# Stage two of an adapter feed-forward kernel: another order on VectorE and ScalarE, and residual rows loaded two chunks later

## The reference

```python
# x (8, 256, 1024); ids (8,), each 3 to 7; weight (8, 1024, 1024)
x1 = einsum('bsi,boi->bso', x, weight[ids])                 # stage one
base_out = einsum('btd,od->bto', x1, base_W) + base_b
logits = einsum('btd,nd->btn', x1, router_W) + router_b     # 15 logits
probs = softmax(logits)
topk_p, topk_i = top_k(probs, 8)
w = topk_p summed by expert_map[topk_i]                     # 8 experts
h = einsum('btd,erd->bter', x1, A)                          # 8 experts x rank 16
lora = einsum('bter,eor->bto', h * w[..., None], Bm) * 2.0
out = x + base_out + lora
```

## Time and profile before

| | us |
|---|---|
| median of 3 runs | 430.16 (429.05 to 432.26) |
| the profiled execution, its own time | 432.55 |
| its span | 430.7 |
| TensorE busy | 404.3 |
| VectorE busy | 295.6 |
| ScalarE busy | 154.9 |

### The profile page before, as it was taken

One profiled execution on the slowest core, in us unless ns is written; L12 is line 12 of the kernel. 1 busy time (PEld: TensorE's weight loads), 2 busy tenths in 40 slices (PEclk: granted clock), 3 DMA queues, 4 the chain that ended last, 5 costly groups with the idle time before them and its releaser, 6 DMA issues.

```text
span 430.7 us, 6373 instructions
## 1 busy us (share of the span) xinstructions
PE 404.3 (94%) x2272; PEld 373.5 (87%) x2272; DVE 295.6 (69%) x577; ACT 154.9 (36%) x238; POOL 0.8 (0%) x8
## 2 busy tenths in 40 slices
PE   6989969998599998999999999999999999999997
PEld 5869869877598898989899898988989898988996
DVE  2586996788736886389844998369863898449643
ACT  3466325571104631166202642056401652035200
POOL 0000000000000000000000000000000000000000
PEclk9999999999599999999999999999999999999999
DMA  6999403771015740276204760157402762055002
GB/s 200 384 299 390 151 1 148 266 226 45 0 50 202 284 147 0 97 278 219 88 0 174 282 226 0 49 218 269 146 0 110 289 211 72 0 195 195 2 2 97
DMA packets 25598, 64.73 MB, mean 150 GB/s; under 512 B 2546, under 2 KB 11634, under 8 KB 25586
## 3 DMA queue, kind: packets, MB, share of 16 engines
q1 hardware_dynamic: 25586, 64.57, 42.4%
HBM read 56.18 MB, written 8.39 MB: 150 GB/s over the span
## 4 chain that ended last, share of the span: by engine, by line
PE 61%; DVE 21%; ACT 6%; issue 6%; DMA 5%; SPq 1%; DVEq 0%; ACTq 0%
PE y_ps L726 22%; PE y_ps L728 11%; DMA w_raw<-in_wT 5%; PE x_ps L761 4%; PE x_ps L763 4%; PE x_ps L762 4%; DVE w_lo L458 3%; ACT w_hi L357 3%; DVE res L555 3%; DVE x_split L464 3%; ACT x_split L367 1%; PE y_ps L738 1%; PE z_ps L762 1%; PE z_ps L761 1%; PE z_ps L763 1%
## 5 line engine op out<-in xcount | busy, mean ns | idle before, releaser
L726 PE MATMUL y_ps<-x_split,w_hi 128*128 128x512 f32 x496 | 173.1, 395 | 3.1 <-DVE y_sum L470 2.9
L728 PE MATMUL y_ps<-x_split,w_lo 128*128 128x256 f32 x496 | 137.6, 277 | 0.0
L726 PEld LDWEIGHTS y_ps<-x_split,w_hi 128*128 128x128 f32 x496 | 93.0, 188 | 25.6 <-issue 3.1
L728 PEld LDWEIGHTS y_ps<-x_split,w_lo 128*128 128x128 f32 x496 | 93.2, 188 | 0.0
L458 DVE TENSOR_TENSOR w_lo<-w_raw,w_hi 128x1024 fp32r<-128x1024 f32 x62 | 75.7, 1224 | 16.5 <-ACT w_hi L357 14.4
L357 ACT CAST w_hi<-w_raw 128x1024 fp32r<-128x1024 f32 x62 | 64.8, 1049 | 14.4 <-DMA w_raw<-in_wT 14.3
L349 ACT COPY y_sum<-y_ps 128x256 f32<-128x256 f32 x62 | 23.1, 372 | 115.7 <-PE y_ps L728 115.7
L470 DVE TENSOR_TENSOR y_sum<-y_ps,y_sum 128x256 f32<-128x256 f32 x62 | 26.1, 421 | 30.3 <-ACT y_sum L349 29.7
L749 PE MATMUL pl_ps<-pl_hi,y_hi 128*128 128x432 f32 x128 | 46.0, 359 | 0.0
L750 PE MATMUL pl_ps<-pl_lo,y_hi 128*128 128x432 f32 x128 | 45.8, 358 | 0.0
L751 PE MATMUL pl_ps<-pl_hi,y_lo 128*128 128x432 f32 x128 | 45.8, 358 | 0.0
(11 more groups left out here) (136 smaller groups left out, 608.0 us busy)
## 6 DMA issues: line engine op xcount, KB each, us to landing
w_raw<-in_wT SPq DMA_DIRECT2D x63, 512.0 KB, 3.3
res<-in_x SPq DMA_DIRECT2D x16, 512.0 KB, 4.2
out<-res SPq DMA_DIRECT2D x15, 512.0 KB, 2.6
x_raw<-in_xT SPq DMA_DIRECT2D x14, 512.0 KB, 6.1
hi_raw<-in_base_t SPq DMA_DIRECT2D x4, 368.0 KB, 6.1
st_raw<-in_base_t SPq DMA_DIRECT2D x4, 368.0 KB, 6.8
pl_raw<-in_base_t SPq DMA_DIRECT2D x2, 576.0 KB, 6.4
x_raw<-in_xT SPq DMA_DIRECT2D x4, 256.0 KB, 4.1
```

Of the source, the lines that this page charges most:

```text
L726: nc.tensor.matmul(y_ps[:, c % 2, :], w_hi[:, s, k, :], x_split[:, k, :, :].rearrange("p s t -> p (s t)"), start=(k == 0), stop=False)
L728: mm = nc.tensor.matmul(y_ps[:, c % 2, 0:T], w_lo[:, s, k, :], x_split[:, k, 0, :], start=False, stop=(k == KC - 1))
```

## The change

VectorE, all elements but 0: the low part of next x (`make_x_lo`) moves from before `fourth_lo` to behind `make_hwt_lo`, so `routing_logits` and the first x_ps add come earlier. In element 1, `fourth` and `routing_logits` go ahead of `add_bias`, and `fourth_lo` goes behind `make_hwt_lo`. ScalarE: `exponential` goes ahead of `make_x_hi`. SyncE: the residual rows are loaded with chunks 4 and 5. In element 0 the splits of the A, router and plain columns come two chunks later, the routing comes straight behind the masks, then bias add and block sums 1 and 2, then `make_hwt_lo`, the low part of Bm, block sums 3 and 4, next x, and the next element's weights. TensorE waits for the low parts of T1, T2, T3 one by one instead of for all three ahead of T1's product.

```diff
                         load_w(this if c + W_SLOTS < OC else nxt, (c + W_SLOTS) % OC)
-                    if c in (2, 3):
-                        load_res(b, c - 2)
+                    if c in (4, 5):
+                        load_res(b, c - 4)
...
                 fourth_hi(b)
+                exponential(b)
                 if not last:
                     make_x_hi(b + 1)
-                exponential(b)
                 make_hwt_hi(b)
...
-                if c == 2:
+                if c == 4:
                     ar_hi()
-                if c in (3, 4):
-                    plain_hi(c - 3)
+                if c in (5, 6):
+                    plain_hi(c - 5)
             for h in range(2):
                 blocks_hi(h)
+            exponential(0)
             make_x_hi(1)
-            exponential(0)
             act.wait_ge(b_in, 16)
             act.wait_ge(ar_lo_done, 2)
             nc.scalar.copy(b_hi[:, :], b_raw[:, :]).then_inc(b_hi_done, 1)
+            make_hwt_hi(0)
             for c in range(OC, OC + 3):
                 adapter_hi(0, c)
-            make_hwt_hi(0)
...
-            def stage2(b):
-                routing_logits(b)
+            def stage2(b, last):
                 dve.wait_ge(res_biased, 2 * b + 2)
                 dve.wait_ge(x_ps_done, x_adds(b, 1))
                 add(0, N1, x_ps[:, 0:NH]).then_inc(x_added, 1)
...
                 make_hwt_lo(b)
+                if isinstance(b, int) and b == 1:
+                    fourth_lo(b)
+                if not last:
+                    make_x_lo(b + 1)
                 dve.wait_ge(x_ps_done, x_adds(b, 3))
...
                     t2_lo()
                     t34_lo()
-                add_bias(b)
-                fourth(b)
-                if not last:
-                    make_x_lo(b + 1)
-                fourth_lo(b)
-                stage2(b)
+                    fourth(b)
+                    routing_logits(b)
+                    add_bias(b)
+                else:
+                    add_bias(b)
+                    fourth(b)
+                    fourth_lo(b)
+                    routing_logits(b)
+                stage2(b, last)
...
-                if c == 2:
+                if c == 4:
                     ar_lo()
-                if c in (3, 4):
-                    plain_lo(c - 3)
+                if c in (5, 6):
+                    plain_lo(c - 5)
             blocks_lo(0)
             blocks_lo(1)
             masks()
-            block_sums_1_2()
-            add_bias(0)
             routing_logits(0)
             routing_gates(0)
-            make_x_lo(1)
+            add_bias(0)
+            block_sums_1_2()
+            make_hwt_lo(0)
             dve.wait_ge(b_hi_done, 1)
             nc.vector.tensor_tensor(b_lo[:, :], b_raw[:, :], b_hi[:, :], ALU.subtract).then_inc(b_lo_done, 1)
+            block_sums_3_4()
+            make_x_lo(1)
             for c in range(OC, OC + 3):
                 adapter_lo(0, c)
-            make_hwt_lo(0)
-            block_sums_3_4()
...
-                pe.wait_ge(t_lo_done, 3)
+                pe.wait_ge(t_lo_done, 1)
                 pe.wait_ge(s_lo_done, KH * (b - 1) + KH)
                 pe.wait_ge(z_added, z_adds(b, 0))
                 product(z_ps, s_block(S1), T1).then_inc(z_ps_done, 1)
+                pe.wait_ge(t_lo_done, 2)
                 pe.wait_ge(x_added, x_adds(b, 1))
                 product(x_ps, s_block(S2), T2, begins=False).then_inc(x_ps_done, 1)
...
+                pe.wait_ge(t_lo_done, 3)
                 pe.wait_ge(x_added, x_adds(b, 2))
                 product(x_ps, s_block(S3), T3, begins=False).then_inc(x_ps_done, 1)
```

## The result

| | before | after |
|---|---|---|
| median, us | 430.39 (429.05 to 432.26) | 415.64 (414.16 to 417.20) |
| the profiled execution, its own time | 432.55 | 415.91 |
| its span | 430.7 | 414.1 |
| TensorE busy | 404.3 | 403.5 |

The medians are of four runs each (the 430.16 us ahead of the prediction was of three). The ratio is 0.966 with a 95% interval of 0.960 to 0.971: faster by 3.4%, 14.8 us by the medians and 16.6 us by the two profiled executions. The same kernel was run and profiled once more, on another chip: a median of 414.54 us beside 430.57 us, and 413.86 us for its profiled execution. In the code after, the stage-one matmuls are L732 and L734, the plain ones L755 to L757, the block products L767 to L769, `lora_b` L781 to L783; the lines of VectorE and ScalarE keep their numbers up to L564.

What follows compares the result with a forecast made beforehand. TensorE, busy 94% of the span, bounds the kernel: its matmuls plus its holes. Gains of 5.8 + 6.2 + 1.8 + 5.3 = 19.1 us from 430.16 give 411.1 us, range 408.5 to 418.0.

Steps and rivals of the forecast that it cites:

- main case: Whole kernel: all terms as forecast, elements 0 and 1 within their bounds; 409 to 414 us, chance 0.62.
- best bounds: Whole kernel: largest gains allowed, 6.7 us in element 0 and 8.5 us in element 1, giving 408.5 us.
- element 1: Element 1 overall: stalls and slow clock fall from 11.1 to 4.9 us; gain 6.2 us, bounds 1.3 and 8.5.
- element 2: Element 2, before the second x_ps product: the 1.50 us hole goes with 0.26 us restart; gain 1.8 us.
- elements 3 to 6: Before the second x_ps product: the 1.06 us hole goes, 1.32 us in each element; gain 5.3 us.
- Steady elements: Elements 2 to 6: x_ps add at about 212.8, before TensorE wants it; moved make_x_lo hidden behind make_hwt_lo.
- Element 0: Plain products 0.9 us earlier, holes before transposes (1.85) and adapter's second product (3.0) go; 5.8 us, bounds 4.0 and 6.7.
- Element 1, stage one: Stage one of element 1: VectorE about 2 us late; 2.1 us of new holes, bounds 1.2 and 3.0.
- Element 1, S2: Element 1, before the second x_ps product: loss 2.8 us instead of 7.07, bounds 1.4 and 4.0.
- Clock: I take none: Element 1: no slow-clock cost after the change, bounds 0 and 2.78 us; before, 2.78 us.
- Residual loads: SyncE's loads two chunks later: no cost in steady elements; element 1's late chunk 7 weights had cost a 1.0 us hole.
- VectorE becomes the limit between elements 0 and 1: Rival: late stage one 1.2, late weights at plain product 1.2, clock drop 2.8 us; 416.3 us, 414 to 418, chance 0.22.

Runs made afterwards that it cites:

- steady-part kernel: Kernel before with only make_x_lo behind make_hwt_lo and ScalarE's exponential first, in elements 2 to 6; 423.38 us, ratio 0.984.
- two kernels: Kernel after with SyncE's adapter numbers read before waiting for element 0's stores, 412.54 us; that plus element 1's first weight load ahead of the second store, 411.39 us.
- element 0 and residual-load kernels: Kernel before with only element 0's new order, 429.14 us; kernel before with only residual rows loaded with chunks 4 and 5, 432.08 us in one run.

## Why the prediction was right where it was, and where not

The forecast was 411.1 us with a range of 408.5 to 418.0; 415.64 us lies in it. It lies outside the 409 to 414 us of the main case, which had the larger chance, and inside the 414 to 418 us of the second. (The range's lower end has a slip: the best bounds sum to 6.7 + 8.5 + 7.1 = 22.3 us, not 21.6.) The sum was 19.1 us, the two profiles show 16.6. Term by term:

| | predicted, us | measured, us |
|---|---|---|
| element 0 | 5.8 | 68.48 - 63.64 = 4.84 |
| element 1 | 6.2 | 60.00 - 55.27 = 4.73 |
| element 2 | 1.8 | 50.44 - 48.68 = 1.76 |
| elements 3 to 6 | 5.3 | 4 x 1.32 = 5.28 |

The first two terms depend on the execution. The second profile of the unchanged kernel after starts element 1 at 62.14 and element 2 at 116.87, so it has 6.34 and 5.27 us for them, 18.7 us in all. And in the steady-part kernel, whose elements 0 and 1 are those of before, element 0 ends at 71.16 and element 1 takes 57.02 us. By the start of element 2 the kernels with the old elements 0 and 1 agree better (128.2 to 128.5 in four profiles): from 128.48 the two terms together are 9.6 and 11.6 us in the two profiles, forecast 12.0.

- **Steady elements: right.** The step counted what stands between the fourth sum and the add. It had the add at 33.9 us behind the start of stage one (212.8 - 178.92) and it came at 33.8 (201.40 - 167.59). That `make_x_lo` is hidden behind `make_hwt_lo` held as well.
- **Element 0: right in mechanism, 1.0 us too high.** The hole before the transposes and the 2.77 us one are gone; 0.58 us is left before the plain product (1.0 was given back in the sum). Chunk 2 started at 16.41 us, 15.82 before, which is the first DMAs and explains 0.6 us; other executions started element 1 at 62.14 (the same kernel) and 64.00 (with the residual loads put back). Alone, this part gives only 1.7 us by the medians.
- **Element 1, stage one: mis-sized.** The sum had 2.1 us of holes with an upper bound of 3.0; it is 2.91 + 0.26 = 3.2, with clock 4.8 us. "SyncE too sends the second store, and then this element's loads, only after the last add of element 0" named the right queue, but gave the reading of the adapter numbers nothing. Before, it was hidden: the store was issued by 69.6, and the load at 71.7 had in any case to wait for the first chunk, done at 71.4. An earlier TensorE took that cover away. VectorE's lateness was real (first y_sum at 68.67) but was not what ended the hole; it then idled 3.74 us. That shortening SyncE's path shortens the hole, to 1.24 and 0.40 us, is shown by two kernels.
- **Element 1, S2: over-priced.** 2.8 us were taken, 1.48 + 0.26 = 1.7 came. VectorE's chain from the T2 split to the end of the add is as forecast: 107.9 - 97.43 = 10.5 us, measured 105.68 - 95.09 = 10.6. But TensorE now wanted that add 104.26 - 95.09 = 9.2 us behind the start of the split, where before it was 105.73 - 97.43 = 8.3. The 0.9 us are the late weights of that one execution before (VectorE waited 3.08 us for them until 87.35), which had pushed VectorE's end of stage one back: in the steady-part, element 0 and residual-load kernels, all with this chain as before, the hole is 5.93, 5.96 and 5.92 us, not 6.81.
- **"Clock: I take none": wrong here.** It rested on one hole of 2.77 us in one execution that no slow stretch followed. The 1.1 us too little for stage one and the 1.1 us too much for S2 cancel, by luck; the 1.5 us by which element 1 falls short of its 6.2 are about the 1.65 us of this term.
- **Residual loads: right that they cost nothing.** That their old place costs the 1.00 us hole is half right: of four profiles with the old place and the old element 0, two have late weights and a hole in that place (1.00 and 0.60 us), two have neither.
- **The base.** Of the 4.5 us between 411.1 and 415.64, 2.5 is the sum as these two profiles have it. The rest comes from taking a sum read in one execution from the median: that execution's own time was 432.55, 2.4 above the median of 430.16, the one after 415.91, 0.3 above its own.

Of the rivals, "VectorE becomes the limit between elements 0 and 1" came in part: the larger hole and its clock drop did, the late weights at the plain product did not. Its sum, 416.3 us, is nearer than the main one. Its name was half right; SyncE was the limit there first.

## What to carry to other kernels

When a change makes one engine start a stage earlier, walk through every other queue between the two stages and price each instruction in it, register reads too: what was hidden there is hidden only as long as that engine starts late. Put instructions that nobody waits for yet behind those that free a buffer; it costs nothing while the engine has idle time further on, and where it has none the wait only moves. A landing time, or a clock that did not fall, read in a single execution is one throw; before a term rests on it, keep the other outcome in the sum.

## What the runs showed of the hardware

**The clock after a hole.** The same 2.77 us hole of element 0 stands in five profiles. Granted clock behind it, in the kernel before and in the steady-part kernel:

```profile
62.00:64.00 2.00, 2.00 (x15) 2.00 (x15) 2.00 (x2) 0.00 (x0) 0.00 (x0) 1.00 0.00 0
```

```profile
62.00:64.00 2.00, 1.29 (x5) 1.32 (x6) 2.00 (x3) 0.00 (x0) 0.00 (x0) 0.72 0.00 0
64.00:66.00 2.00, 2.00 (x9) 2.00 (x8) 2.00 (x3) 0.14 (x1) 0.00 (x0) 0.50 0.00 0
```

It fell to 0.50 in four of the five. Of the holes in element 1, those of 2.51, 2.63, 2.91 and 3.23 us were followed by 0.50, those of 2.54 and 3.02 us were not; all four of 5.9 to 6.8 us were, and none of those of 1.0 to 1.6 us. So between 2.5 and 3.2 us the length of the hole does not decide it. The Trainium skill, TensorE: Matmul & The Clock Gate, "What's actually happening", has the gate's look at activity run freely, so that the point at which the clock changes varies from run to run. These profiles agree with it; they don't show the cause.

**GpSimd and VectorE.** While GpSimd added two SBUF operands (3260 ns for 128x1024, VectorE needs 1.2 us for it), VectorE's splits of two SBUF operands took 3.40 and 2.75 us for 1.23 and 0.55. The Trainium skill, SBUF — State Buffer, "Who interferes with whom", says that a VectorE instruction with two SBUF inputs and a GpSimd instruction that reads SBUF exclude each other for a whole instruction; the 2.2 us added to each agrees.

**Loads.** The same load of 512 KB of weights landed in 3.2 to 4.3 us, or, between two loads of residual rows, in 5.5 to 6.3 us in five of seven profiles and in 3.4 and 3.7 us in the other two. In the changed kernel the first load of element 1, issued at 71.24 with none before it, landed in 3.4 us, the two issued behind it by 73.4 in 4.5 and 4.7 us.
